# Three-part splits kept in PSUM with TensorE taking off the rounded parts, and value biases folded into output bias rows

## The reference

```python
x = LN(x + self_attn0(x))            # q,k,v from one in-projection, out = ctx @ Wo.T + bo
x = LN(x + cross_attn0(x, ctx))      # q Wq+bq, k Wk+bk, v Wv+bv
x = LN(x + routed_ffn(x))            # 16 experts, top 1, plus a shared FFN
x = LN(x + self_attn1(x))            # rope on q and k, causal, out = ctx @ wo_w + wo_b
x = LN(x + cross_attn1(x, ctx))      # 16 heads of 16, out = concat @ Wo + bo
x = LN(x + tree_ffn(x))              # 255 sigmoid routers, 256 leaves, out @ Wout.T + b

# in self_attn1
q = apply_rope((x @ wq_w + wq_b).reshape(b, l, 16, 16))
k = apply_rope((x @ wk_w + wk_b).reshape(b, l, 16, 16))
v = (x @ wv_w + wv_b).reshape(b, l, 16, 16)
# rope: [first*cos - second*sin, second*cos + first*sin]
# in cross_attn1
qh = (q @ Wq + bq); kh = (k @ Wk + bk); vh = (v @ Wv + bv)
```

## Time and profile before

| what | us |
| --- | --- |
| median of 3 runs (lowest, highest) | 1765.05 (1759.35, 1765.16) |
| span of the profiled execution | 1755.5 |
| PE, DVE, ACT, POOL busy in it | 1545.8, 1107.1, 791.1, 304.7 |
| l0_attn | 0 to 211.3 |
| experts, with the first gate and up projections | 465 to 643 |
| combine_and_prepare | 654.2 to 763.0 |
| heads_tail t3 | 944.1 to 1003.7 |
| heads_tail t4 | 1652.2 to 1693.2 |
| l1_tree | 1693.2 to 1755.5 |

### The profile page before, as it was taken

The page is one execution under the profiler, slowest core; times in us unless marked ns, Lnnn a source line. Parts: engine busy times, 40 slices in busy tenths (PEclk is TensorE's granted clock), DMA queues, the critical chain, the costliest instruction groups (busy, mean ns, idle before and its releaser), DMA issues. The chain is left out here.

```text
span 1755.5 us, 28756 instructions
## 1 busy us (share of the span) xinstructions
PE 1545.8 (88%) x8850; PEld 841.1 (48%) x8850; DVE 1107.1 (63%) x2286; ACT 791.1 (45%) x1566; POOL 304.7 (17%) x323
## 2 busy tenths in 40 slices
PE   6776689987999979759899699999999999999876
PEld 3444357873599966424445323333333323332355
DVE  4778515553122217957775699887878878886256
ACT  2333214431111101336664327776767767777522
POOL 3555500003000016710002420000000000000141
PEclk9987789998999989979999869998999989999998
DMA  9544410003599942763334612222232222220001
GB/s 338 162 133 139 139 30 1 1 10 111 177 328 334 330 143 79 251 192 98 96 97 112 199 29 57 57 57 58 60 92 65 68 58 57 57 57 1 1 1 48
DMA packets 178018, 189.77 MB, mean 108 GB/s; under 512 B 12171, under 2 KB 157231, under 8 KB 177906
## 3 DMA queue, kind: packets, MB, share of 16 engines
q1 hardware_dynamic: 170092, 172.14, 32.6%
q0 software_dynamic: 4080, 12.33, 1.9%
q10 hardware_dynamic: 3734, 3.83, 0.7%
HBM read 129.65 MB, written 58.34 MB: 107 GB/s over the span
## 5 line engine op out<-in xcount | busy, mean ns | idle before, releaser
L1772 DVE TENSOR_REDUCE xa_part<-psum 128x1 f32<-128x401 f32 (+1 forms) x1024 | 512.4, 567 | 91.2 <-PE psum L1646 85.6
L1747 ACT ACTIVATE xa_P<-psum 128x512 f32<-128x512 f32 (+1 forms) x832 | 434.2, 600 | 160.9 <-PE psum L1671 160.9
L1646 PE MATMUL psum<-xa_K,sa_Q 96*128 96x401 bf16 (+1 forms) x1024 | 328.1, 353 | 9.8 <-PEq L1809 9.4
L1671 PE MATMUL psum<-sa_Q,xa_K 98*128 98x512 bf16 (+1 forms) x832 | 319.4, 390 | 14.4 <-issue 7.7
L1684 PE MATMUL psum<-xa_P,xa_V 128*32 128x512 f32 (+1 forms) x1664 | 226.3, 616 | 0.1
L1671 PEld LDWEIGHTS psum<-sa_Q,xa_K 98*128 98x128 bf16 (+1 forms) x832 | 81.8, 100 | 271.8 <-ACT xa_P L1747 192.7
L1646 PEld LDWEIGHTS psum<-xa_K,sa_Q 96*128 96x128 bf16 x1024 | 102.6, 100 | 102.8 <-DVE xa_part L1772 33.1
L1772 DVE TENSOR_REDUCE sa_part<-psum 128x1 f32<-128x128 f32 (+3 forms) x256 | 113.7, 487 | 59.0 <-PE psum L1649 57.8
L1747 ACT ACTIVATE sa_P<-psum 128x512 f32<-128x512 f32 (+3 forms) x256 | 101.1, 440 | 54.3 <-PE psum L1674 51.6
L118 POOL TENSOR_TENSOR x_sb<-x_sb,x_bo_sb 128x256 f32<-128x256 f32 x16 | 11.6, 750 | 632.4 <-SPq L1809 632.4
L1239 PE MATMUL psum<-xtT,wgu 128*128 128x128 f32 x992 | 115.9, 275 | 1.6 <-ACT xtT L1275 1.6
(11 more groups left out here) (221 smaller groups left out, 2226.4 us busy)
## 6 DMA issues: line engine op xcount, KB each, us to landing
wgu<-in_f_gu SPq DMA_DIRECT2D x31, 1024.0 KB, 7.5
xa_K<-kx SPq DMA_DIRECT2D x96, 200.1 KB, 4.5
wdn<-in_f_dn SPq DMA_DIRECT2D x31, 512.0 KB, 7.7
vx<-xv_v SPq DMA_DIRECT2D x48, 256.0 KB, 3.2
xa_V<-vx SPq DMA_DIRECT2D x16, 768.0 KB
sa_Q<-qs SPq DMA_DIRECT2D x16, 384.0 KB, 3.7
sa_K<-ks SPq DMA_DIRECT2D x16, 384.0 KB, 4.6
sa_Q<-qx SPq DMA_DIRECT2D x16, 384.0 KB, 3.8
```

The lines of the kernel that those rows point to most:

```text
L1646: last = pe.matmul(o, Qst[0:QK_ROWS, u, h, qt * P:(qt + 1) * P], Kst[0:QK_ROWS, u, h, k0:k1], start=True, stop=not causal)
L1671: last = pe.matmul(o[0:r, 0:w_], Kst[0:ONE + 2, u, h, kt * P:kt * P + r], Qst[0:ONE + 2, u, h, q0(kt):L], start=True, stop=not causal)
L1747: act.activation(Pr[0:r, (u * KT + kt) % R, h, 0:w_], ring2(1 + u * S1 + pos(g, n))[0:r, 0:w_], ACT.Exp, scale=SCALE).then_inc(s_exp, 1)
L1772: dve.tensor_reduce(part[:, h * TB + qt, e:e + 1], ring1(n)[:, 0:k1 - k0], AX, ALU.max).then_inc(s_1free, 1)
```

## The change

Both kinds of split now keep the value in PSUM until its last part is rounded. ACT rounds hi, mid and lo straight from PSUM, with the bias each time for xk and xq. Between them PE takes the rounded part off: a matmul of the bf16 part with minus the identity (`negb`) added into the same PSUM region (`take`, 512 columns at most, so two matmuls for 800 or 801 columns and one for 512). The passes of DVE for the rest and of POOL for lo are gone. With rope, DVE adds ta and tb back into the block's own PSUM (`dve_whole`), in place of POOL's sum, and waits first for both halves' products. `freed` now waits for `s_lo`, the last rounding.

Values are copied without their bias by ACT in both blocks. Their bias is multiplied with the output matrix instead and joined with the output bias: three rows (for t3, t4 and the tree's tail) are computed in the experts' block by 8 float32 matmul passes of 256 columns for 3 rows and a chain of 8 DVE operations which splits them in three bf16 parts (`split_rows`); `down` waits for them (`s_b3`). `pe_proj` adds a row to each tile by one matmul of three ones with the three parts, and `pool_residual` is gone. The output bias of l0_attn joins the split of its input bias (1024 columns in place of 768; the first projection waits for three loads in place of two). `l0_attn`, `combine_and_prepare` and `heads_tail` have new orders on PE and ACT.

```diff
@@ class Split
     def freed(self, pe, n):
-        pe.wait_ge(self.s_rot if self.rope else self.s_rest, n + 1)
+        pe.wait_ge(self.s_lo, n + 1)
+    def round(self, act, n, j, ps):
+        w_ = self.width_of(n)
+        if self.rope:
+            return act.activation(self.parts[:, n % self.ring, j, 0:w_], ps, ACT.Copy)
+        return act.activation(self.parts[:, n % self.ring, j, 0:w_], ps, ACT.Identity, bias=self.bias(n))
...
+    def act_mid(self, act, n, ps):
+        act.wait_ge(self.s_sub1, n + 1)
+        self.round(act, n, 1, ps).then_inc(self.s_mid, 1)
+    def act_lo(self, act, n, ps):
+        act.wait_ge(self.s_sub2, n + 1)
+        self.round(act, n, 2, ps).then_inc(self.s_lo, 1)
+    def take(self, pe, n, j, ps):
+        w_ = self.width_of(n)
+        for q in range(0, w_, BANK):
+            e = min(q + BANK, w_)
+            last = pe.matmul(ps[:, q:e], self.env.negb, self.parts[:, n % self.ring, j, q:e], start=False, stop=True,
+                             skip_group_check=True)
+        return last
+    def pe_sub1(self, pe, n, ps):
+        pe.wait_ge(self.s_hi, n + 1)
+        self.take(pe, n, 0, ps).then_inc(self.s_sub1, 1)
+    def pe_sub2(self, pe, n, ps):
+        pe.wait_ge(self.s_mid, n + 1)
+        self.take(pe, n, 1, ps).then_inc(self.s_sub2, 1)
...
+    def dve_whole(self, dve, n, ps):
+        dve.wait_ge(self.s_rot, n - n % 2 + 2)
+        dve.tensor_tensor(ps, self.ta[:, n % 2, :], self.tb[:, n % 2, :], ALU.add).then_inc(self.s_whole, 1)
@@ Tail.pe_proj
             for k in range(self.kc):
                 last = pe.matmul(self.ps(1, c)[:, i * D:(i + 1) * D], lhs(i, k), w(k),
-                                 start=(k == 0), stop=(k == self.kc - 1))
+                                 start=(k == 0), stop=(k == self.kc - 1 and self.bias is None))
+            if self.bias is not None:
+                last = pe.matmul(self.ps(1, c)[:, i * D:(i + 1) * D], self.env.ones3, self.bias, start=False, stop=True)
@@ l0_attn, PE
                     last.then_inc(val.s_full, 1)
+                    keys.pe_sub1(pe, p, K_PS)
...
                     pair(4 * c)
                     if ahead:
                         project(c + 1, 1)
+                    keys.pe_sub2(pe, 4 * c, K_PS)
                     pair(4 * c + 1)
...
@@ combine_and_prepare, PE
+                    for n in blocks_at(c - 1):
+                        sp_.pe_sub1(pe, n, half(n))
                     if 2 <= c < CHUNKS + 2:
                         tail.pe_out(pe, c - 2)
+                    for n in blocks_at(c - 1):
+                        sp_.pe_sub2(pe, n, half(n))
                     for n in blocks_at(c):
...
@@ combine_and_prepare, ACT
+                    for n in blocks_at(c - 1):
+                        sp_.act_hi(act, n, half(n))
                     if 2 <= c < CHUNKS + 2:
                         tail.act_out(act, c - 2)
                     for n in blocks_at(c - 1):
-                        sp_.act_mid(act, n)
-                    for n in blocks_at(c):
-                        sp_.act_hi(act, n, None)
+                        sp_.act_mid(act, n, half(n))
+                    for n in blocks_at(c - 1):
+                        sp_.act_lo(act, n, half(n))
+                    if len(blocks_at(c)) and blocks_at(c)[-1] % 4 == 3:
+                        b = blocks_at(c)[-1] // 4
+                        val.act_copy(act, b, pair(3 * b + 2))
```

281 lines of the change are left out of this document (125 added, 156 removed).

## The result

| | before | after |
| --- | --- | --- |
| median of 4 runs each (lowest, highest), us | 1762.20 (1757.98, 1765.16) | 1821.13 (1814.43, 1824.02) |
| ratio, 95% interval | | 1.0339 (1.0308 to 1.0369) |
| span of the profiled execution, us | 1755.5 | 1820.2 |

What follows compares the result with a forecast made beforehand. A chain over PE, ACT and DVE was taken to bound l0_attn, with combine_and_prepare deciding. Terms -4 + 1.8 + 27.7 + 1 - 2.6 + 0.7 = +24.6 gave span 1780.1, plus 9.5 to the median: 1790 us, range 1768 to 1813.

Steps and rivals of the forecast that it cites:

- The rest is taken as it stands: Both heads loops, experts' gate and up products, l0_xattn, routing and shared FFN: same instructions, so no term in the sum.
- l0_attn, -4 forecast: First chunk +2, two full chunks -1.3 each, last -3; PE and ACT chain binds; bounds -12 and +8 (lower clock).
- the last chunk, forecast at -3: l0_attn's last chunk, without projections: DVE binds and gains its contention and rests, 4.2 us at most, taken as -3.
- Ahead of the experts, +1.8: Eight float32 passes at 0.23 us on PE before the first gate products; the wait at the first `down` is hidden.
- combine_and_prepare, +27.7 forecast: The deciding term: longer holding of PSUM +17.7 us and bursts at the lower clock +10; bounds +15 to +59.
- the +10: combine_and_prepare: seven more bursts beginning at the lower clock, 1.6 us each, make 11.3, of which +10 us is taken.
- the +17.7 for the chain: combine_and_prepare at full clock: steps of 21.9 us against 13.47, more beside the tail; end at 780.2 against 762.5.
- Tails and tree, -0.9 forecast: t3 +1 for roundings and subtractions, t4 -2.6 for DVE's faster apply less bias matmuls, tree +0.7 for bias matmuls.
- B: Rival, chance 0.15: no change that can be told; no burst slows, l0_attn gains its whole bound; +4, 1769 us.
- C: Rival, chance 0.08: faster; DVE bounds l0_attn and POOL's absence frees it, if the chain is under 36.6; -25, 1739 us.
- D: Rival, chance 0.12: much slower; every burst in combine_and_prepare runs at the lower clock end to end; +56, 1821 us.
- A: The forecast, chance 0.65: longer holding of PSUM in combine_and_prepare costs 15 to 35 us, the rest cancels; 1773 to 1800.

Runs made afterwards that it cites:

- b_pad52: Kernel before with 52 increments of an unused semaphore on PE's list ahead of the cross-attention (xa) loop: 1780.33 us, ratio 1.0112.
- e1_pad16: Changed kernel with 16 increments of an unused semaphore on PE's list ahead of the cross-attention (xa) loop: 1782.78 us, ratio 1.0132.
- e7_kfirst: Changed kernel with k blocks ahead of the q blocks' subtractions on PE in combine_and_prepare, values copied after k's roundings: 1801.25 us, ratio 1.0225.
- e8_align: Changed kernel with 64 bytes of each partition left empty ahead of the heads' buffers, no instruction changed: 1811.94 us, ratio 1.0292.
- e2_comb_old: Changed kernel with the old splits and value copies on DVE without bias in combine_and_prepare alone: 1786.90 us, ratio 1.0143.

## Why the prediction was wrong in size

**"The rest is taken as it stands."** This is the step that failed. It passed over two loops with the same instructions, 829 us of the span. The change put 52 instructions (modulo 256) more on PE's list ahead of the xa loop, which is enough to add a second standstill of 3.2 to 3.5 us to the one of 2.5 to 2.7 behind each of three jumps, and low clock behind them: +13.0. b_pad52 shows this with the kernel before, and the packets of the instruction queue show what PE waits for. The row of the kernel before that says "2.48 <- issue" at the first jump was in the trace before the prediction, and I did not ask what it was. The sa loop's +8.9 is of the same sort, the same instructions and another time, but its cause isn't settled.

**l0_attn, -4 forecast, +7.9 measured.** The chain was right: a pair of 8.40 us against 8.4, chunks of 44.7 and then 47.8 (sum to sum) against 42.6, and DVE no longer bounds (it waits 17.4 to 20.5 us for each sum). Three sizes were off. The bias matmul was put at 0.15 us a tile, from its columns; it is 0.35 from start to start: about 0.8 a chunk. The lower clock, which stood in the bounds (+8), fell on the third output projection (2.08 us for what takes 1.13) and on parts of the chunks. And the last chunk, forecast at -3 because DVE would bind there, was bound by a chain as well: the next hi stands on ACT behind the attention's exp, which waits for DVE. This is ACT's list at that place, in the changed kernel:

```profile
174.03 0.42 ACT L583 ACTIVATE ex<-sc 128x256 f32<-128x256 f32 x1 [5.22 <-DVE sc L635]
174.35 0.91 ACT L269 ACTIVATE xk_parts<-psum,x_bk_sb 128x800 bf16<-128x800 f32 x1
```

What the clock costs can be read from chunks of identical instructions. Six kernels have this l0_attn with its two middle chunks unchanged. These twelve chunks took 43.0 us at a granted clock of 1.00 (one), 44.6 to 44.7 at 0.96 (four), 46.1 and 46.2 at 0.93, and 47.8 at 0.89 (five), and PE's busy time grew by the same amount. The two ends of this row, a chunk of e1_pad16 and one of the changed kernel:

```profile
69.70:112.71 43.01, 34.47 (x132) 19.81 (x134) 25.45 (x39) 19.44 (x24) 1.04 (x1) 1.00 0.42 134
114.37:162.16 47.79, 39.28 (x133) 22.19 (x136) 25.46 (x40) 19.44 (x24) 1.02 (x1) 0.89 0.38 120
```

At the full clock the chunk is 43.0 us against the 42.6 of the forecast. The last chunk took 40.5 us at 0.87 (e1_pad16) and 47.8 at 0.68 (four kernels); before the change it took 44.3 at 0.69. So the last chunk had the low clock already before; with the change its length follows it both ways, 3.8 us less or 3.5 more. In e1_pad16 the whole of l0_attn took 207.1 us, which would have made the term -4.2, the forecast. That the sums agree so closely is in part luck: there the first chunk is 0.4 us longer where 2 was forecast, the second middle one 0.1 longer where 1.3 less was forecast, and the last one 3.8 shorter instead of 3. In the four other profiles of the same instructions l0_attn took 218.7, 219.2, 222.2 and 222.2 us (e7_kfirst, after, e8_align and e2_comb_old), at clocks of 0.88 and 0.87. The 12 us between them and e1_pad16 go with the clock; why it is granted differently to the same instructions is open.

**Ahead of the experts, +1.8.** The eight passes stand between 475.63 and 477.45: 1.82 us. No wait for s_b3 followed. Right; the 0.23 us of one, taken from a row, held. (The stage grew by only 1.3: it varies by more than that.)

**combine_and_prepare, +27.7 forecast, +25.3 measured.** Here both the waits and the clock came out as forecast. The steps from q blocks to q blocks were 25.4, 26.1 and 27.7 us. The first had no low burst, and 25.0 or 26.2 was forecast for a step with a projection of the tail. Less what their low bursts have above 3.60 us, the second is 24.3 (the other of these two figures was forecast) and the third, which has no projection, 23.4, forecast 23.4. The low bursts were longer than forecast (5.4 to 6.0 us against 5.3) but four and not seven: 8.2 us against the +10. The rest of the +25.3, 17.1 us, stands against the +17.7 for the chain. Two smaller errors lie inside: more time for a low burst against fewer of them.

**Tails and tree, -0.9 forecast, +7.7 measured.** Again the bias matmul. In t3 two tiles take 2.52 us, from 991.28 to the turn at 993.80, and took 1.81 before (947.32 to 949.13): 0.35 a tile, 16 tiles, 5.7 us for a forecast term that did not contain them at all. The timeline of PE in t3:

```profile
991.28 1.11 PE L145 MATMUL psum<-s_wo_sb,t_cT 128*128 128x256 f32 x4
992.32 0.28 PE L148 MATMUL psum<-rows,ones 3*128 3x256 bf16 x1
992.53 1.13 PE L145 MATMUL psum<-s_wo_sb,t_cT 128*128 128x256 f32 x4
993.59 0.28 PE L148 MATMUL psum<-rows,ones 3*128 3x256 bf16 x1
```

In t4 the forecast had half of the bias matmuls at 1.2 us; at 0.35 a tile all sixteen are 5.7 us beside DVE's forecast gain of 3.8, and the stage came out at -0.3. The tree's +2.9 was not followed further, and the stage took 59.2 to 62.3 us in kernels that have no bias matmul.

**The rivals.** B and C are refuted: DVE's relief came in full (147.5 to 109.2 us busy in l0_attn) and bought nothing, because PE and ACT bound the chunk. D named 1821 and the kernel takes 1821, but not by D's mechanism: every burst at the lower level would take 7.0 us (3.60 + 3.44), and the longest took 5.97. That D's number came out is luck. (C's condition, a chain under 36.6 us, is worked out nowhere; by C's own sum it would be DVE's 32.9. Neither is met.) A's mechanism held at the place where A put it. The Trainium skill ("TensorE: Matmul & The Clock Gate", section "HAM oscillation — how this bites in real kernels") tells of short bursts that fall back to the slow clock; the trace agrees in part, in half of the eight bursts, each for only a part of its length, and the last chunk of l0_attn, where I had not looked for it, runs at 0.68 (and at 0.69 before).

## What to carry to other kernels

A change that adds or removes instructions ahead of a loop moves the loop's code; before two kernels are compared, look at the first instructions behind each jump back for a wait for "issue" and at the packets of the instruction queue, and put idle instructions where the engine waits anyway until both are down. Keeping a tile in PSUM through several roundings trades passes of two idle engines for a longer chain over the two that share the tile: count the chain from "tile full" to "tile free", and order the other engine's work into it (here half of the loss). A tiny matmul between large float32 ones is to be costed by the time from start to start of its neighbours, not by its own columns.

## What the hardware showed that was not expected

- The same loop of 1690 instructions on PE took 631 to 635, 648 or 660 to 662 us by the place of its code alone, in steps of none, one or two standstills (2.3 to 2.9 and 2.9 to 3.8 us) behind a jump back, and lower clock behind them.
- With standstills the loop's code was fetched anew in each round (68 to 70 instruction packets of 16384 bytes in the whole program); without them three rounds of 1690 instructions passed with no packet at all (41 to 43).
- A bf16 matmul with 3 rows of weights and 256 columns, its busy time 0.28 us, cost 0.35 us between float32 matmuls, in l0_attn (1.27 us a tile) as in t3.
- An increment of a semaphore on PE takes 0.17 us: 80 of them made t3's stretch 13.9 us longer.
- Twelve chunks of identical instructions took 43.0, 44.7, 46.1 or 47.8 us, and the granted clock of each (1.00, 0.96, 0.93, 0.89) orders them without exception.
